# Second cross-attention: eight of thirteen key chunks summed on GpSimd instead of nine, one pair of maximum matmuls in each free gap, and the output update later in GpSimd's queue

## What is computed

```python
x = x + jnp.tanh(g_xattn[1]) * _L1_xattn_ref(_layernorm(x, axis=-1), ctx_2048)

def _L1_xattn_ref(qkv, y):
    N_HEADS = 16
    bs, width, length = qkv.shape            # 4, 512, 512
    ch = width // N_HEADS                    # 32
    q = qkv.reshape(bs * N_HEADS, ch, length)
    k = v = y.reshape(bs * N_HEADS, ch, -1)  # 1601 keys
    scale = 1.0 / math.sqrt(math.sqrt(ch))
    weight = jnp.einsum('bct,bcs->bts', q * scale, k * scale)
    weight = jax.nn.softmax(weight, axis=-1)
    a = jnp.einsum('bts,bcs->bct', weight, v)
    return a.reshape(bs, -1, length)
```

## Time and profile before

| what | value |
|---|---|
| median of 3 runs | 1976.45 us (1969.62 to 1991.58) |
| the profiled execution | 1985.32 us, span 1983.5 us |
| second cross-attention with slots 0 to 15 | about 788 to 1705 us of the span |
| busy shares over the span | PE 82%, DVE 59%, ACT 43%, POOL 45% |
| mean granted clock of PE | 0.938 of full speed |

### The profile page before, as it was taken

The page is one execution under the profiler, slowest core; times in us unless marked ns, Lnnn a source line. Parts: engine busy times, 40 slices in busy tenths (PEclk is TensorE's granted clock), DMA queues, the critical chain, the costliest instruction groups (busy, mean ns, idle before and its releaser), DMA issues. The chain is left out here.

```text
span 1983.5 us, 21889 instructions
## 1 busy us (share of the span) xinstructions
PE 1636.2 (82%) x7412; PEld 606.7 (31%) x7440; DVE 1179.3 (59%) x1538; ACT 848.6 (43%) x1273; POOL 897.8 (45%) x340
## 2 busy tenths in 40 slices
PE   5999997996676766888888887888888888699898
PEld 3444443443333321222222222122222221244443
DVE  3878999883444547766655566555566550344543
ACT  1221212113566541566665656565666666311110
POOL 0012254422443243766666787566787667300000
PEclk9999998998898885999999999899999998799999
DMA  9240323223344443122222112222112224000000
GB/s 331 63 155 6 94 78 96 89 90 132 101 135 126 132 138 79 37 61 61 61 61 61 26 37 61 62 61 61 26 38 60 61 50 88 1 0 21 21 21 22
DMA packets 141003, 144.04 MB, mean 73 GB/s; under 512 B 60238, under 2 KB 110690, under 8 KB 140902
## 3 DMA queue, kind: packets, MB, share of 16 engines
q1 hardware_dynamic: 128998, 105.99, 20.2%
q10 hardware_dynamic: 11904, 36.74, 5.7%
HBM read 99.73 MB, written 23.88 MB: 62 GB/s over the span
## 5 line engine op out<-in xcount | busy, mean ns | idle before, releaser
L1510 ACT ACTIVATE c_prob<-c_scores,ctx_scales 128x512 f32<-128x512 f32 (+1 forms) x832 | 533.0, 684 | 388.8 <-PE c_scores L1562 286.1
L1426 DVE TENSOR_REDUCE c_piece_max<-c_unit 128x1 f32<-128x804 f32 x512 | 479.9, 982 | 299.0 <-PE c_unit L1545 294.3
L1366 POOL TENSOR_TENSOR c_prob_sum<-c_prob_sum,c_prob 128x2048 f32<-128x2048 f32 x112 | 506.6, 4523 | 12.0 <-POOL c_prob_sum L1366 6.7
L1545 PE MATMUL c_unit<-c_khigh,c_qdiag 128*128 128x402 f16 x1024 | 265.8, 352 | 120.9 <-DVE c_piece_max L1426 104.2
L1562 PE MATMUL c_scores<-c_queries,c_keys 97*128 97x512 f16 (+1 forms) x832 | 300.3, 398 | 61.7 <-ACT c_prob L1510 51.7
L1571 PE MATMUL c_out<-c_prob,c_VT 128*32 128x512 f32 (+1 forms) x1664 | 233.9, 636 | 0.1
L676 PE MATMUL a_S<-a_ctxT,a_xnT 128*128 128x401 f32 x512 | 190.3, 516 | 7.2 <-ACT a_prob L633 3.9
L1562 PEld LDWEIGHTS c_scores<-c_queries,c_keys 97*128 97x128 f16 (+1 forms) x832 | 72.1, 99 | 385.4 <-ACT c_prob L1510 325.7
L706 PE MATMUL a_o<-a_ctx,a_probT 128*128 128x512 f32 (+1 forms) x416 | 183.5, 598 | 0.0
L1545 PEld LDWEIGHTS c_unit<-c_khigh,c_qdiag 128*128 128x128 f16 x1024 | 79.2, 99 | 270.2 <-DVE c_piece_max L1426 210.1
L1366 POOL TENSOR_TENSOR c_prob_sum<-c_prob 128x2048 f32<-128x2048 f32 x16 | 72.4, 4526 | 172.4 <-ACT c_prob L1510 143.3
(11 more groups left out here) (197 smaller groups left out, 1941.8 us busy)
## 6 DMA issues: line engine op xcount, KB each, us to landing
c_keys<-key_parts SPq DMA_DIRECT2D x48, 400.5 KB, 4.2
b_k<-in_keys ACTq DMA_DIRECT2D x16, 801.0 KB, 6.1
a_ctx<-in_ctx SPq DMA_DIRECT2D x12, 1024.0 KB, 6.7
c_VT<-in_values SPq DMA_DIRECT2D x16, 768.0 KB
a_ctxT<-in_ctxT SPq DMA_DIRECT2D x12, 802.0 KB, 4.9
key_parts<-b_khigh ACTq DMA_DIRECT2D x16, 400.5 KB, 2.9
key_parts<-b_krest ACTq DMA_DIRECT2D x16, 400.5 KB, 4.4
c_khigh<-key_parts SPq DMA_DIRECT2D x16, 400.5 KB, 3.8
```

What stands on the lines that cost most here:

```text
L1366: nc.gpsimd.tensor_tensor(psum4[:], a[:], prob[(j * MC + c) % RING][:], ALU.add).then_inc(sums_taken, 2 if i == 1 else 1)
L1426: nc.vector.tensor_reduce(piece_max[j % 2][:, k // 2, k % 2:k % 2 + 1], U[bank(unit)][:, :, 0:PIECE], axis=AX.XY, op=ALU.max).then_inc(uni ...
L1510: nc.scalar.activation(prob[(j * MC + c) % RING][0:w, h, :], STp[h % 2][0:w, :], ACT.Exp, scale=score_scale[0:w]).then_inc(exp_done, 1)
L1545: last = nc.tensor.matmul(U[bank(unit)][:, e, 0:PIECE], QZ[o][:, h, t * P:(t + 1) * P], khigh[o][:, at:at + PIECE], start=True, stop=True)
```

## The change

`POOLED` has eight chunks instead of nine: the chunks 4, 6 and 9 leave it and 7 and 10 come in, so a slot has seven additions on POOL and 19 blocks on PE. `add_gain` stands after POOL's fifth addition instead of the first. The four reciprocal parts stand ahead of DVE's units 3, 5, 7 and 9. And the account of costs goes: the 33 gaps without a block get the 33 units, one each (in slot 0, which has 49 units, up to two).

```diff
-        POOLED = [0, 1, 2, 3, 4, 5, 6, 8, 9]
+        POOLED = [0, 1, 2, 3, 5, 7, 8, 10]
...
                 add_up(g, j, 1)
-                if not isinstance(g, int) or g > 0:
-                    add_gain(g - 1)
                 add_up(g, j, 2)
                 add_up(g, j, 3)
                 add_up(g, j, 4)
                 add_up(g, j, 5)
+                if not isinstance(g, int) or g > 0:
+                    add_gain(g - 1)
                 add_up(g, j, 6)
                 if later:
                     normalize(g + 3)
                 add_up(g, j, 7)
-                add_up(g, j, 8)
...
-                    if before and 3 <= u < 3 + PARTS:
-                        finish(g - 1, u - 3)
+                    if before and u in range(3, 3 + 2 * PARTS, 2):
+                        finish(g - 1, (u - 3) // 2)
...
-                BLOCK, PAIR = 1.25, 0.36
-                per_gap = (BLOCK * len(gaps) + PAIR * max(len(stream), UNITS)) / (H * MC)
-                given, done = 0, 0.0
+                free_gaps = H * MC - len(gaps)
+                given = passed = 0
...
                     if what:
-                        done += BLOCK
-                    upto = (gap - 3) * per_gap
-                    while given < len(stream) and (done + PAIR / 2 <= upto or gap == 4 * MC + 3):
+                        return
+                    passed += 1
+                    upto = len(stream) if passed == free_gaps else passed * max(len(stream), free_gaps) // free_gaps
+                    while given < min(len(stream), upto):
                         unit = stream[given]
                         if unit[0] == "rows" and gap < ROWS_GAP:
                             break
                         rows(unit) if unit[0] == "rows" else pair(unit)
                         given += 1
-                        done += PAIR
```

More of the change, by code:

```diff
@@ L1615, in slot @@
                 gaps = placed(before)
-                BLOCK, PAIR = 1.25, 0.36
-                per_gap = (BLOCK * len(gaps) + PAIR * max(len(stream), UNITS)) / (H * MC)
-                given, done = 0, 0.0
+                free_gaps = H * MC - len(gaps)
+                given = passed = 0
                 def products(gap):
-                    nonlocal given, done
+                    nonlocal given, passed
                     what, b = gaps.get(gap, (None, None))
```

## The result

The changed kernel takes 1836.1 us (median of 4 runs, 1834.09 to 1838.04) against 1974.74 us before: the ratio is 0.928, with a 95% interval of 0.923 to 0.934. The profiled execution took 1834.49 us, its span is 1832.7.

What follows compares the result with a forecast made beforehand. PE's work bounds the second cross-attention once linked DVE and POOL waits go: slot 43.9 + 3.1 + 0.2 = 47.2 us. Savings of 131.1 + 5 + 10.9 + 7.3 = 154 us off 1976.45 give 1822 us, range 1793 to 1868.

Steps and rivals of the forecast that it cites:

- The slot: Second cross-attention, loop slot: from 58.07 us to 47.2, as PE work 43.9, pair stalls 3.1 and 0.2 at gap 10.
- seven runs of three: Single pairs in three neighbouring gaps, seven times a slot: PE stalls 0.44 us each for DVE, 3.1 us per slot.
- The term for gap 10: Gap 10 of a slot, where ACT's `split_queries` holds back an exponential: 0.2 us added.
- POOL's queue: POOL's additions in a slot: fifth ends at 27.3 us, sixth at 34.5; every wait for POOL goes.
- three waits: Second cross-attention: PE for DVE's maxima (104 us), ACT for POOL's additions (94), POOL for the reciprocals (80), called linked.
- Rival (c): Release does little, the slot being bound by a loop through ACT: slot 55.9 + 1.1, total 1948 us; chance 0.02.
- The ring: ACT's refill behind POOL's additions: nearest is chunk 12, needing its addition at 37.2 us against 34.5, 2.7 to spare.
- The new `den` wait: Chunk 4's `den` in gap 23 waits for the fourth reciprocal: 3 us to spare, price nothing to 1 us per slot.
- The clock: Granted clock in loop slots: falls assumed to go with the waits; if they stay, +2.2 us per slot.
- (a): Clock still falls once a slot: +2.2 us in each of 13 slots, total 1851 us; chance 0.13.
- (d): Short PE stalls before pairs keep the clock low much of the stage: at half, slot 65 us, total 2056; chance 0.03.
- The sum: Savings: slots 1 to 13 131.1 us, slot 0 5, slot 14 10.9, slot 15 7.3; 154 together, off median 1976.45.

Runs made afterwards that it cites:

- even: Changed kernel with a slot's blocks placed by a table so that no three gaps without a block stand in a row: 1818.49 us, ratio 0.918.
- a_deal: Changed kernel with the old dealing of pairs in bunches; eight pooled chunks, late output update and spread reciprocals stay: 1939.11 us, ratio 0.981.
- b_deal: Kernel before with only the dealing changed: single pairs and spread reciprocals, nine pooled chunks and early output update kept: 1965.71 us, ratio 0.992.
- a_pool9: Changed kernel with nine pooled chunks again instead of eight: 1860.19 us, ratio 0.942.
- a_gain1: Changed kernel with the output update (`add_gain`) right after the first addition again: 1904.94 us, ratio 0.966.
- a_recip: Changed kernel with the four reciprocals ahead of units 3, 4, 5 and 6 again: 1836.05 us, ratio 0.927.
- b_gain5: Kernel before with only the output update moved behind the fifth addition; nine pooled chunks and bunched pairs stay: 1944.27 us, ratio 0.982.
- b_again: Kernel before, unchanged, profiled a second time: 1977.28 us.
- even2: Changed kernel with the evenly placed blocks and the first two output blocks one gap earlier (gaps 9 and 12): 1805.14 us, ratio 0.911.

## Why the prediction was right, and where its sum was off

**The slot.** 47.2 us were worked out, 47.14 were measured. Its terms stand one by one: the gap with a pair 0.58 (1089.51 to 1090.09), the gap with a block 1.31 (1091.69 to 1093.00), seven runs of three with 1.60 from first to third pair. The term for gap 10 was put at 0.2 and is 0.07. The runs are shown by even: without them PE doesn't wait for DVE. POOL's queue came out as laid out too: its fifth addition ends 27.2 us into the slot (27.3 forecast), the sixth 34.4 (34.5).

**The limits.** That POOL and DVE hold the slot together was argued from three waits. The table of combinations shows it: with the bunches alone in place the slot is 53.5 to 55.5 us (a_deal), with POOL's queue alone 55.2 to 56.7 (b_deal), so the waits could not be added up; what counted was PE's own sum after both had gone. Rival (c), a slot that stays at 55.9 + 1.1, is refuted. The ring had 2.7 us to spare for the sixth addition by the prediction; a_pool9 shows that an addition more is already late by 1.74.

**The new `den` wait.** It was put at 3 us to spare. The fourth reciprocal on DVE's timeline and the block on PE's, in the changed kernel:

```profile
1098.44 0.95 DVE L1444 RECIPROCAL c_rden<-c_den 128x128 f32<-128x128 f32 x1
```

```profile
1101.12 1.06 PE L1582 MATMUL c_den<-c_prob,c_ones 128*32 128x512 f32 x8
```

That is 1.7 us, and no wait. The error of 1.3 us is the same one that made a_gain1 dearer than expected: the fourth reciprocal stands behind the maximum of unit 8, which can't begin before 1097.53, when its pair is there. With the early placing it ends 3.8 us sooner (a_recip, 9.0 instead of 12.8 us behind `den_of_sum`), at the same total, so the wait is covered either way.

**The clock.** Windows of the slots 1 to 13, of the kernel before and of the changed one (length, busy us of PE, PEld, DVE, ACT, POOL, granted clock, DMA):

```profile
853.15:1604.46 751.31, 618.30 (x3433) 159.59 (x3432) 449.87 (x530) 456.48 (x716) 527.63 (x179) 0.97 0.22 53
```

```profile
851.01:1469.41 618.40, 591.49 (x3537) 165.00 (x3537) 459.17 (x531) 455.96 (x716) 469.17 (x166) 0.99 0.27 64
1469.41:1552.57 83.16, 74.73 (x433) 16.82 (x436) 21.67 (x25) 61.93 (x100) 68.42 (x18) 0.96 0.33 74
```

The falls went with the waits, as the forecast took it, and rivals (a) and (d) with them: PE is busy for 591 of 618 us and holds the upper level but for one fall at the step of the loop. The forecast had no price for a fall, only the bound of 2.15 us between slot 1 and slot 6 of the kernel before. Both of these have a fall (granted clock 0.97), and slot 1 is no longer than slot 2, which has none (55.92 and 55.91 us). Two neighbouring slots of the loop, 10 and 11, give a price:

```profile
1377.69:1435.75 58.06, 47.74 (x265) 12.32 (x265) 34.72 (x41) 35.11 (x56) 40.66 (x14) 0.97 0.22 53
1435.75:1492.29 56.54, 46.24 (x265) 12.24 (x264) 34.61 (x41) 35.15 (x56) 40.68 (x14) 1.00 0.22 54
```

a_deal and b_gain5 have the same step between slots with and without a fall (55.45 and 53.86, 55.93 and 54.33). So some 1.5 of the 11 us that such a slot of the loop gained are clock. That the falls would go was assumed in the forecast and not worked out; it came true. The experiments don't settle which waits bring a fall: where ACT waits for POOL 2.5 to 5 times a slot (a_gain1, b_deal) the clock falls in every slot, but in the kernel before, with as many, not in the slots 2, 11 and 12; without such waits it falls in five of the eleven slots (a_deal, b_pool8) or in two (b_gain5), and with the single wait of 1.7 us in a_pool9 in none.

The Trainium skill (TensorE: Matmul & The Clock Gate, Part 1) states that the throttled clock is the default and activity releases it; the trace agrees with that, with 591 of 618 us busy and 0.99. The oscillation that its section "A second HAM failure mode: psum-queue depth-cycling" describes didn't come, with 93 stalls of PE for DVE between 850 and 1520 us.

**The sum.** On the profiled execution the terms were 131.1 + 5 + 10.9 + 7.3 = 154 us; measured are 132.9 for slots 1 to 13, 4.9 for slot 0 (60.2 us from 790.86 to 851.01, where 59.6 were worked out), 10.1 and 5.2, 153.1 in all. The execution as a whole is 150.8 us shorter, as the stage begins 2.8 us later than before. Slot 15 is 2 us longer than forecast, and its start, and the end of slot 14, run at the lower level: a block of 1.94 us at 1513.64. In a_deal, where the clock is 1.00 throughout slot 15, it takes 36.70 us, the 36.8 of the forecast. The step of the loop costs 5.3 instead of 6.6.

**The term that was mis-sized** is the last one: I took the whole saving, worked out on an execution of 1985.3 us, off the median of 1976.45, and got 1822 where 1836.1 came out. What made that execution long was not a constant beside the change but time in the very slots that the change shortens, where the clock fell more: b_again has 744.7 + 50.1 us there instead of 751.3 + 54.4, so against it only 126.3 + 5.9 us are saved. The changed kernel has no such surplus to lose. That makes 8.9 of the 13.7 us; 3.2 are savings that were put too high (154 against 150.8), and 1.6 is the distance of the changed kernel's profiled execution from its median. Had I set the new stage as I had worked it out, 700.5 us, into an execution of median length like b_again, the forecast would have been about 1834.

## What to carry to other kernels

Add up what the fullest engine has to do by start-to-start times of stretches without a wait, and add only those waits that the new order still must have; a list of waits by releaser can't be summed when each limit covers the other. When two limits lie close together, each fix alone looks poor (34, 39 and 13 us of some 140), so judge them together. And take a saving off the same execution that it was worked out on: a surplus over the median may stand in the part that is about to go.

## What the runs showed of the hardware

Two things that I had not expected. Two executions of the same kernel differ by 11 us in 14 slots, and the slots come in steps: 55.9 us outside the loop, 56.5 in it at the full clock (1.00) and 58.1 with a fall (0.97). With the waits gone they are 47.1 in both profiles, and nine runs of the changed kernel span 7 us (1830.67 to 1838.04) where 33 of the kernel before span 22 (1969.62 to 1991.58). And the clock still falls in the last two slots, which have no pairs: PE waits there 0.56 and 0.19 us once per chunk, the granted clock is 1.00 from 1490 to 1510 us all the same, and then 0.67 and 0.65 in the two windows of 5 us from 1510 to 1520. After that it stays at the upper level to the end of slot 15 with the same waits, and in a_deal, even and even2 there is no fall in the slots 14 and 15 at all (1.00). What makes the difference I did not find out.
